# Mamba and FFN block: skip term by scaled transposes, norm shift on ScalarE, 12 states on GpSimd, ends rewritten

## The reference, cut to what matters

```python
xz = einsum('btd,pd->btp', x, W_xproj)              # 96 columns: rank 64, B 16, C 16
dt = softplus(einsum('btr,dr->btd', xz[..., :64], W_dt) + b_dt)
A = -exp(A_log)
h = exp(dt * A) * h + dt * B * x                    # scan over tokens, per channel and state
y = einsum('bds,bs->bd', h, C) + Dp * x             # Dp * x is the skip term
x = layernorm(x + y)
gate, up = x @ wg.T, x @ wu.T                       # hidden size 768, weights int / 127
x = layernorm(x + (silu(gate) * up) @ wd.T)
```

## Time and profile before

| | |
|---|---|
| median of 3 runs | 1906.5 us (1903.86 to 1908.56) |
| the profiled execution | 1904.62 us, its span 1902.8 us |
| TensorE / its weight loads | 1703.2 / 1339.9 us busy |
| VectorE | 1754.1 us busy |
| ScalarE | 1599.5 us busy |
| GpSimd | 1639.2 us busy |
| granted TensorE clock | 0.984 of full speed in the mean |

### The profile page before, as it was taken

How to read it: one execution, slowest core, us unless ns; L and a number is a source line. 1 busy time by engine, 2 the same in 40 slices (tenths; PEclk the granted TensorE clock), 3 DMA queues, 4 the chain that set the end, 5 groups by cost and what they waited for, 6 DMA issues and landing times. The chain is left out here.

```text
span 1902.8 us, 33164 instructions
## 1 busy us (share of the span) xinstructions
PE 1703.2 (90%) x11048; PEld 1339.9 (70%) x11048; DVE 1754.1 (92%) x2060; ACT 1599.5 (84%) x2992; POOL 1639.2 (86%) x710
## 2 busy tenths in 40 slices
PE   5789999998999999999998999989999999999977
PEld 3566777776777776777776777766777777777765
DVE  4999999999999999999999999999999999999993
ACT  5879898898888889898898888889888898888863
POOL 5988999898899988999898899988999898899960
PEclk9999999999999999999999999999999999999989
DMA  7322444233443232444232444233444233443200
GB/s 240 128 93 76 141 135 136 83 108 100 141 135 129 96 100 103 140 135 137 83 113 96 141 135 130 96 99 102 141 135 135 81 110 101 141 135 118 73 12 23
DMA packets 107419, 216.51 MB, mean 114 GB/s; under 512 B 10129, under 2 KB 44530, under 8 KB 107250
## 3 DMA queue, kind: packets, MB, share of 16 engines
q1 hardware_dynamic: 107250, 214.39, 34.7%
HBM read 195.48 MB, written 18.87 MB: 113 GB/s over the span
## 5 line engine op out<-in xcount | busy, mean ns | idle before, releaser
L408 POOL TENSOR_TENSOR h<-h,c_bc 128x1024 f32<-128x1024 f32 x352 | 830.3, 2368 | 122.3 <-ACT h_carry L490 62.3
L398 POOL TENSOR_TENSOR ub<-u,b_bc 128x1024 f32<-128x1024 f32 x320 | 753.3, 2368 | 0.1
L504 ACT ACTIVATE p_da<-dt,neg_a 128x512 f32<-128x512 f32 x640 | 435.1, 683 | 126.9 <-DVE h L699 121.2
L922 PE MATMUL p_y<-ident,h 128*128 128x128 f32 x4096 | 530.4, 278 | 5.2 <-POOL h L408 3.8
L922 PEld LDWEIGHTS p_y<-ident,h 128*128 128x128 f32 x4096 | 478.5, 144 | 37.6 <-issue 19.8
L699 DVE TENSOR_TENSOR_SCAN h<-p_da,h_carry,ub 128x512 f32<-128x512 f32 x320 | 392.6, 1264 | 6.6 <-ACT p_da L504 4.3
L699 DVE TENSOR_TENSOR_SCAN h<-p_da,ub 128x512 f32<-128x512 f32 x320 | 375.7, 1206 | 20.3 <-ACT p_da L504 13.0
L977 PE MATMUL p_o<-wt_down,hid 128*128 128x256 f32 x1536 | 347.3, 379 | 2.4 <-DVE res L740 1.6
L518 ACT ACTIVATE ub_t<-u_t,bc_t 128x256 f32<-128x256 f32 x768 | 341.6, 496 | 0.0
L977 PEld LDWEIGHTS p_o<-wt_down,hid 128*128 128x128 f32 x1536 | 286.8, 190 | 53.1 <-issue 14.7
L896 PE MATMUL p_da<-ident,ub_t 128*128 128x128 f32 x1536 | 236.2, 278 | 79.3 <-ACT ub_t L518 49.0
(11 more groups left out here) (91 smaller groups left out, 1642.4 us busy)
## 6 DMA issues: line engine op xcount, KB each, us to landing
c_bc<-bc_rows_dram SPq DMA_DIRECT2D x352, 256.0 KB, 6.3
b_bc<-bc_rows_dram SPq DMA_DIRECT2D x64, 768.0 KB, 6.7
b_bc<-bc_rows_dram SPq DMA_DIRECT2D x64, 512.0 KB, 3.6
x_in<-in_L_attn_x SPq DMA_DIRECT2D x32, 512.0 KB, 7.3
out_x<-res_n SPq DMA_DIRECT2D x32, 512.0 KB, 3.5
bc_rows_dram<-bc_rows SPq DMA_DIRECT2D x32, 64.0 KB, 1.6
hid<-in_L_ffn_w_gate SPq DMA_DIRECT2D x1, 768.0 KB, 5.1
hid<-in_L_ffn_w_up SPq DMA_DIRECT2D x1, 768.0 KB, 6.8
```

The costliest lines, as they stand in the source:

```text
L398: nc.gpsimd.tensor_tensor(ub[:, i % UB_SLOTS, :, :], u[:, par, :, :], b_bc[:, i:i + 1, :].broadcast_to([P, DH, T]), ALU.mult).then_inc(s_u ...
L408: nc.gpsimd.tensor_tensor(h[:, s % H_SLOTS, :, :], h[:, s % H_SLOTS, :, :], c_bc[:, i:i + 1, :].broadcast_to([P, DH, T]), ALU.mult).then_i ...
L504: nc.scalar.activation(da, dt[:, par, q, :], ACT.Exp, scale=neg_a[:, q, s:s + 1]).then_inc(done, 1)
L922: ins = nc.tensor.matmul(p_y_tok[:, k, q * P:(q + 1) * P], h[:, s % H_SLOTS, q, k * P:(k + 1) * P], ident[:, :], start=(s == SUM_ORDER[0] ...
```

## The change

- **States.** `POOL_STATES` gets 5 and 12 and loses 13, 12 in all, so VectorE multiplies states 6, 8, 13 and 15 by C. `K_STATES` stays at six: 7 and 13 for 9 and 14. `K_SLOTS` 3 for 2, `UB_SLOTS` 4 for 5; the slots now go on round from chunk to chunk.
- **Skip.** ScalarE makes x_s = (Dp + 1) * x_t in two pieces of 128x512 (`x_scaled0`, `x_scaled1`, at state 2 of its own chunk), and TensorE adds it with eight transposes. `skip_diag` is gone.
- **Norm shift.** VectorE only negates the means (`negate`, 8 columns), which does not wait for rstd; ScalarE makes the shift in eight activations of one column, input neg_mean, scale rstd.
- **Order.** Most places in `AT` move by some zones; u_of from state 7 to 8; norm_log and norm_exp a state earlier, in ScalarE's list ahead of norm1; `LATE` 9 for 13, `STORE_AT` 4 for 11. The carry is made one state later, at zone 0, behind that zone's other jobs.
- **Waits.** `first_wait` leaves out a wait for a value that this engine has waited for before.
- **Start.** VectorE makes u and the first ub of chunk 0.
- **Tail.** The last chunk's hidden values go to free h buffers; four gates come before the last piece of the down projection of the chunk before; ScalarE's silus come before the second norm of that chunk; the last norm and store are done in two halves.

The core of the diff (the reordering in `AT` is given by the list above and the lines that the prediction speaks of):

```diff
-POOL_STATES = (0, 1, 2, 3, 4, 7, 9, 10, 11, 13, 14)
+POOL_STATES = (0, 1, 2, 3, 4, 5, 7, 9, 10, 11, 12, 14)
+CARRY_LAG = 1
+CARRY_ZONE = 0
 AT = {
...
-    "softplus_log": (5, 3), "dt_of": (7, 0), "u_of": (7, 0), "u_transposed0": (12, 2), "u_out0": (14, 0),
-    "u_transposed1": (14, 3), "u_out1": (14, 2), "z_out": (2, 0), "stats1": (4, 0), "mean1": (5, 1),
-    "norm_log": (6, 0), "norm_exp": (6, 0), "shifts": (6, 1), "norm1_0": (6, 2), "norm1_1": (7, 1),
-    "norm1_2": (7, 1), "norm1_3": (7, 1), "x1_transposed": (8, 0), "x1_high": (8, 0), "x1_low": (8, 2),
-    "gate0": (9, 3), "gate1": (9, 3), "gate2": (10, 1), "gate3": (10, 2), "gate4": (10, 2), "gate5": (10, 2),
-    "silu0": (9, 1), "silu1": (9, 1), "silu2": (9, 2), "silu3": (10, 0), "silu4": (10, 0), "silu5": (10, 0),
-    "exp_table": (10, 0), "up0": (10, 2), "up1": (10, 2), "up2": (13, 0), "up3": (13, 1), "up4": (13, 4),
-    "up5": (14, 3), "hidden0": (11, 0), "hidden1": (11, 0), "hidden2": (13, 1), "hidden3": (14, 0),
+    "softplus_log": (7, 0), "dt_of": (7, 2), "u_of": (8, 1), "u_transposed0": (12, 1), "u_out0": (14, 0),
+    "u_transposed1": (14, 3), "u_out1": (15, 0), "z_out": (2, 1), "stats1": (4, 1), "mean1": (4, 2),
+    "norm_log": (5, 2), "norm_exp": (5, 3), "negate": (6, 0), "shifts": (6, 1), "norm1_0": (7, 0),
+    "norm1_1": (7, 1), "norm1_2": (7, 2), "norm1_3": (7, 2), "x1_transposed": (8, 0), "x1_high": (8, 1),
+    "x1_low": (8, 2), "gate0": (9, 2), "gate1": (9, 3), "gate2": (10, 1), "gate3": (10, 1), "gate4": (10, 2),
+    "gate5": (10, 2), "silu0": (9, 0), "silu1": (9, 0), "silu2": (10, 1), "silu3": (10, 1), "silu4": (10, 1),
+    "silu5": (10, 1), "exp_table": (10, 1), "up0": (10, 2), "up1": (10, 2), "up2": (10, 3), "up3": (12, 2),
+    "up4": (14, 1), "up5": (14, 1), "hidden0": (10, 2), "hidden1": (10, 2), "hidden2": (13, 0),
...
+    "hidden3": (13, 1), "hidden4": (15, 0), "hidden5": (15, 0), "skip0": (13, 0), "skip1": (8, 4),
+    "x_scaled0": (2, 0), "x_scaled1": (2, 2), "down0": (0, 2), "down1": (0, 3), "down2": (1, 1),
...
-K_STATES = (2, 6, 9, 10, 14, 15)
+K_STATES = (2, 6, 7, 10, 13, 15)
-K_SLOTS = 2
-LATE = 13
-STORE_AT = 11
-DA_LEAD = {6: 2, 9: 3, 10: 2, 14: 2}
-UB_SLOTS = 5
+K_SLOTS = 3
+LATE = 9
+STORE_AT = 4
+DA_LEAD = {6: 3, 7: 3, 10: 2}
+UB_SLOTS = 4
...
+            def x_scaled(c, par, q):
+                act.wait_ge(s_xt, c + 1)
+                if first_wait(act, s_skip, 2 * c):
+                    act.wait_ge(s_skip, 2 * c)
+                nc.scalar.mul(x_s[:, q, :], x_t[:, par, q, :], skip1[:, q:q + 1]).then_inc(s_xs, 1)
...
+            def shifts(call, norms=range(2), tiles=range(TT)):
+                act.wait_ge(s_rstd, call)
+                act.wait_ge(s_neg, call)
+                for n in norms:
+                    for t in tiles:
+                        ins = nc.scalar.activation(shift[:, n, t:t + 1], neg_mean[:, n, t:t + 1], ACT.Identity,
+                                                   scale=rstd[:, n, t:t + 1])
+                ins.then_inc(s_ln, 1)
...
-                        if core and par == 0 and zone == 3:
-                            carry(c, s)
+                        if zone == CARRY_ZONE:
+                            cq, sq, pq = unit_at(c, s, -CARRY_LAG, par)
+                            if pq == 0 and (core if s >= CARRY_LAG else prev):
+                                carry(cq, sq)
...
-                nc.vector.scalar_tensor_tensor(shift[:, k, :], mean_var[:, k, :, 0], -1.0, rstd[:, k, :],
-                                               ALU.mult, ALU.mult).then_inc(s_ln, 1)
+            def negate(call, c1, c2, k=slice(0, 2)):
+                wait(dve, s_mean[0], c1)
+                wait(dve, s_mean[1], c2)
+                wait(dve, s_ln, call - 1)
+                nc.vector.tensor_scalar_mul(neg_mean[:, k, :], mean_var[:, k, :, 0], -1.0).then_inc(s_neg, 1)
...
             dt_of(0, 0)
+
+            dve.wait_ge(s_dt, 1)
+            dve.wait_ge(s_xt, 1)
+            nc.vector.tensor_tensor(u[:, 0, :, :], dt[:, 0, :, :], x_t[:, 0, :, :], ALU.mult).then_inc(s_u, 1)
+            dve.wait_ge(s_u, 1)
+            dve.wait_ge(s_b[0], 16)
+            nc.vector.tensor_tensor(ub[:, 0, :, :], u[:, 0, :, :], b_bc[:, 0:1, :].broadcast_to([P, DH, T]),
+                                    ALU.mult).then_inc(s_ub_first, 1)
...
             def skip(c, par, a):
+                if a == 0:
+                    pe.wait_ge(s_xs, 2 * (c + 1))
                 for k in range(2 * a, 2 * a + 2):
                     for q in range(DH):
-                        nc.tensor.matmul(p_y_tok[:, k, q * P:(q + 1) * P],
-                                         x_t[:, par, q, k * P:(k + 1) * P], skip_diag[:, q, :],
-                                         start=False, stop=False, skip_group_check=True)
+                        ins = nc.tensor.matmul(p_y_tok[:, k, q * P:(q + 1) * P],
+                                               x_s[:, q, k * P:(k + 1) * P], ident[:, :],
+                                               start=False, stop=False, is_transpose=True, skip_group_check=True)
+                ins.then_inc(s_skip, 1)
```

More of the change, by code:

```diff
@@ L242, in wait, with first_wait @@
         def wait(eng, s, value):
-            if not isinstance(value, int) or value > 0:
+            if value > 0:
                 eng.wait_ge(s, value)
+        waited = {}
+        def first_wait(eng, s, value):
+            first = value > waited.get((eng, s.name), 0)
+            if first:
+                waited[eng, s.name] = value
+            return first
         def units(c, s):
@@ L259, in k_units, with ub_slot, k_slot, slot_freed @@
             return NK * c + (K_STATES.index(s) + 1)
+        def ub_slot(c, i):
+            return (NB * c + i) % UB_SLOTS
+        def k_slot(c, i):
+            return (NK * c + i) % K_SLOTS
+        def slot_freed(eng, states, c, i, slots):
+            n = len(states) * c + i - slots
+            if n >= 0:
+                value = DH * units(n // len(states), states[n % len(states)])
+                if first_wait(eng, s_scan, value):
+                    eng.wait_ge(s_scan, value)
         def unit_at(c, s, k, par):
@@ L332, in broadcast_b @@
                 i, n = B_STATES.index(first), last + 1 - first
-                if not (isinstance(c, int) and c == 0):
+                if c > 0:
                     wait(sp, s_ub, NB * (c - 1) + i + n)
@@ L359, in step @@
                     broadcasts(c, par, LATE, 2 * N)
-                if nxt and not (isinstance(c, int) and c + 2 >= CHUNKS):
+                if nxt and c + 2 < CHUNKS:
                     load(c + 2)
@@ L371, in tail @@
                 store(c - 1)
[L372 removed]
+                for a in range(2):
+                    sp.wait_ge(s_out_ready, TT * (c + 1) + 2 * (a + 1))
+                    sp.dma_start(out_chunks[c][:, 2 * a:2 * a + 2, :],
+                                 res_n[:, 2 * a:2 * a + 2, :]).then_inc(s_out, 16)
             over_chunks(sp, step, tail)
[L374 removed]
+            sp.wait_ge(s_out, 16 * (CHUNKS + 2))
         @block.gpsimd
@@ L587, in step @@
                             x_out(c + 1, 1 - par)
+                        for q in range(DH):
+                            if core and due(f"x_scaled{q}"):
+                                x_scaled(c, par, q)
                         if nxt and due("rank_out"):
@@ L602, in step @@
                             softplus_log(c + 1, 1 - par)
+                        if (prev or last) and due("norm_log"):
+                            norm_log(c, c if prev else 0, c - 1 if last else 0)
+                        if (prev or last) and due("norm_exp"):
+                            norm_exp(c)
+                        if (prev or last) and due("shifts"):
+                            shifts(c)
                         for k in range(TT):
@@ L637, in tail @@
                 norm_exp(c + 1, slice(0, 1))
+                shifts(c + 1, range(1))
                 for k in range(TT):
@@ L640, in tail @@
                 x1_high(c)
+                for j in range(NH):
+                    silu(c, j, tail_ps[j % 4], tail_hid)
+                exp_table()
                 norm_log(c + 2, 0, c, slice(1, 2))
                 norm_exp(c + 2, slice(1, 2))
-                for j in range(NH):
-                    silu(c, j, tail_ps[j % 4])
+                shifts(c + 2, range(1, 2))
                 for k in range(TT):
                     norm2(c - 1, c + 2, k)
-                exp_table()
-                norm_log(c + 3, 0, c + 1, slice(1, 2))
-                norm_exp(c + 3, slice(1, 2))
-                for k in range(TT):
-                    norm2(c, c + 3, k)
+                for a in range(2):
+                    act.wait_ge(s_mean[1], c + 1 + a)
+                    half = slice(2 * a, 2 * a + 2)
+                    nc.scalar.activation(log_var[:, 1, half], mean_var[:, 1, half, 1], ACT.Ln,
+                                         bias=eps[:, :]).then_inc(s_log_var, 1)
```

(10 more changed lines are left out.)

233 lines of the change are left out of this document (134 added, 99 removed), and 7 rows, old and new, of the table AT.

## The result

1984.03 us (median of 4, 1979.06 to 1987.41) against 1905.78 before (median of 4): ratio 1.0415, 95% interval 1.0402 to 1.0428. The forecast was 1867, range 1834 to 1897. The profiled execution has a span of 1977.3 us.

A forecast was written before the change was run, and what follows sets the result against it. VectorE sets the 57.02 us period, its work plus a wait for TensorE. Per chunk 1.12 + 0.14 - 0.25 = 1.01, times 32 is 32, plus ends 5: 1904.6 - 37 = 1867.6, stated as 1867; range 1834 to 1897.

The forecast's parts named there:

- the price of the negation: VectorE's negation of 8 columns: between 182 and 1486 ns, upper end taken, saving only the 0.14 us wait for rstd.
- a full queue swallows GpSimd's wait for dt: GpSimd's 2.4 us wait for dt a chunk covers its added 2.3 us product, so that product costs nothing.
- the twelfth state: One more product with C on GpSimd, leaving VectorE four instead of five: 1.12 us a chunk off VectorE.
- the scaled transposes: Skip on TensorE as eight transposes: 1.1 us a chunk saved there, nothing off the period.
- GpSimd's cover: GpSimd's 5.9 us of waiting a chunk absorb its extra product, 2.3 us, taking its work to 53.5 us.
- rival 3: GpSimd becomes the bound at 57.0 us a chunk, only the ends are won: 1900 us; chance 0.14.
- Rival 4: ScalarE's scan waits do not shrink, so it runs late: 58.1 us a chunk, 1935 us, slower; chance 0.10.
- the sign that I gave for it: ScalarE's waits for scans above 1.6 us a chunk would show that ScalarE, running late, makes the kernel slower.
- The late carry: Carries on ScalarE come some 1 us later for GpSimd in even chunks, hidden behind its queue: zero cost.
- The up-projection: VectorE's wait for TensorE there stays at 2 us a chunk, bounds 1.2 and 2.3.
- Ends: Start of the kernel 1.5 us earlier (2.4 at best) and tail 3.5 us shorter, together 5 us.
- Rival 2: VectorE's negation runs in 0.16 us beside GpSimd; 1.8 us a chunk off, 1842 us; chance 0.22.

The follow-up runs named there:

- the reduction's run: The changed kernel with VectorE's negation of the means made by a one-element tensor_reduce instead of tensor_scalar: 1870.86 us, ratio 0.9825 to the kernel before.
- the added wait: The changed kernel with GpSimd's step 6 held until VectorE's negation of that chunk is done: 1873.78 us, ratio 0.9841 to the kernel before.
- the kernel before with this one edit: The kernel before, with VectorE negating the means by tensor_scalar and ScalarE making the shift in eight one-column activations: 1962.93 us, ratio 1.0308.

## Why the prediction was wrong, step by step

- **The step that failed** is the price of the negation. I wrote that 182 ns is "the lower bound; the shift's own 1486 is the upper", and took the upper end as nothing saved. It measured 5455. Against the reduction's 134 ns the negation's wait is 5.3 us of VectorE a chunk and 109 us of span (1977.3 less 1868.5); the rest of the 165 us would have been other waits: VectorE's idle time is 3.9 us a chunk in the reduction's run and 2.5 in the changed kernel (400 to 1600 us). The mechanism was named, GpSimd's use of the same way; its size was not, since I took "a wait for GpSimd's operation to end" where, in odd chunks, it is a wait for its ready operations to end. A mean of 31 was read where the single ones lay apart.
- **The step that made it large** I had costed at a gain: that a full queue swallows GpSimd's wait for dt. In odd chunks that wait was what let VectorE through. The change put dt and its product further behind the negation, so that four operations, the running one among them, stand before them where one stood. No run moved these places alone; the shift back on VectorE and the added wait are what bear it out.
- **The period without the lock** came out near: 56.2 and 1870.86 us in the reduction's run, forecast 56.0 and 1867. That is partly luck, for the terms erred both ways. From 400 to 1600 us VectorE works 52.3 us a chunk there, 2.1 less than before, where I had 1.1: the shift's 1.5, which I had kept, is down to 0.13. It is idle 3.9, up by 1.3, where I had 0.1: 1.2 for the carry of state 8 and 0.5 for ScalarE's softplus and high part of x1 are new, 0.5 at the up-projection is gone. Changed one at a time, the twelfth state is worth 1.5 a chunk and the scaled transposes 0.4, waits included; I had 1.12 and 0.
- **GpSimd's cover** held: in the reduction's run its wait for dt is 0 and it waits 2.8 us a chunk in all (45.4 for carries, 13.8 for scans), so rival 3 is out.
- **ScalarE.** Eight shifts pack into 1.59 us, 1.5 in effect, for the 1.2 taken; x scaled 709 ns each as taken. Behind VectorE's long negation it stood 105 us; where the negation is quick it keeps up. Rival 4's mechanism is real, as the kernel before with this one edit shows. But the sign that I gave for it fails: ScalarE's waits for scans stay at 3.2 us a chunk in the reduction's run (69.1 in 1200), far above 1.6, and the period is still 56.2, because its other waits, which I had kept at 3.6, fall to 1.5 (z 3.1 us for 25.0, gates 21.3 for 33.5) and its work is 51.4 for 52.1.
- **The late carry** I put at zero, hidden behind GpSimd's queue. GpSimd's waits for carries hardly changed (45.4 us for 44.6 from 400 to 1600); new is VectorE's, in its product of state 8, some 2.6 us in even chunks. With early carries it went and the time stayed, since the up-projection took what it gave.
- **The up-projection** stayed, at 1.5 us a chunk in the reduction's run for the forecast 2, within its bounds of 1.2 and 2.3; in the changed kernel it is 1.1, below them.
- **Ends.** The start gave 2.0 us at the second joining of dt (49.74 to 47.71), taken 1.5; the first scan itself starts 4.2 us earlier (22.73 for 26.96), more than the 2.4 that I called the best; the tail from the last z copy to the end 42.2 us for 45.8, 3.6, taken 3.5.
- **Rival 2** had the negation at under 0.3 us. With the reduction it is, and the time is not 1842: the other waits take what it gives.

## What to carry to other kernels

Before a small VectorE instruction is priced beside a busy GpSimd, look at its single durations and at where they end, not at their mean: if they end when GpSimd runs dry, the price is its backlog, and an operation moved to GpSimd or past that point can raise it. Give such an instruction a form that does not need the shared way (here a reduction over one element, 134 ns for 5455), or let GpSimd wait once. An idle gap that looks like slack may be what lets another engine through.

## What the runs showed of the hardware that I had not expected

A VectorE instruction that needs what GpSimd holds can be passed over at GpSimd's boundaries: the running operation and three more went by at a pitch of 2.30 us while it waited 8.66. When GpSimd's products were tied to late carries, it passed at the first boundary in all chunks but the first, 1.8 to 2.3 us. The same 8 columns by another instruction form, from and to the same buffers, did not wait at all (134 ns).
